# The expert stage of a routed feed-forward kernel: straight-line experts replaced by a looped body with a two-tile weight ring

## The reference, cut to what matters

```python
probs = softmax(xr @ Wg); gate_vals, expert_idx = top_k(probs, 2)      # 2048 tokens, 8 experts
C = ceil(1.25 * S * K / E)                                             # 640 slots an expert
dispatched = xr[dispatch_mask.reshape(-1) % S].reshape(E, C, d)        # rows of each expert
h = relu(einsum('ecd,edf->ecf', dispatched, w1))                       # w1: 8 x 512 x 2048, float32
expert_out = einsum('ecf,efd->ecd', h, w2)                             # w2: 8 x 2048 x 512, float32
out = einsum('ks,ksm->sm', combine_weights, rerouted); x = x + out     # two experts a token, gated
```

## Time and profile before

| What | Value |
|---|---|
| median of 3 runs | 1315.84 us |
| span of the profiled execution | 1310.3 us (5.5 us under the median, which has what lies around the span) |
| first part and routing | to 475 us |
| expert stage | 475 us to the end |
| instructions executed | 14966 |

### The profile page before, as it was taken

One profiled execution on the slowest core, in us unless ns is written; L12 is line 12 of the kernel. 1 busy time (PEld: TensorE's weight loads), 2 busy tenths in 40 slices (PEclk: granted clock), 3 DMA queues, 4 the chain that ended last, 5 costly groups with the idle time before them and its releaser, 6 DMA issues.

```text
span 1310.3 us, 14966 instructions
## 1 busy us (share of the span) xinstructions
PE 1061.0 (81%) x5058; PEld 837.0 (64%) x5059; DVE 656.6 (50%) x1010; ACT 488.9 (37%) x842; POOL 303.5 (23%) x242
## 2 busy tenths in 40 slices
PE   1055878877998359998997899999698994999895
PEld 0022335434465349997996799888586883988784
DVE  6989899899835223333332233334243432333342
ACT  5354736655644213322222222334243331233242
POOL 4767646476322300002001100100202002000202
PEclk9997997888899569998999899999798997999898
DMA  7051350220023341116221532163534332411441
GB/s 255 20 155 33 116 152 1 64 97 32 2 97 113 138 172 65 65 65 149 90 104 13 140 107 87 19 200 123 141 130 107 137 129 39 170 65 65 92 178 22
DMA packets 64617, 129.23 MB, mean 99 GB/s; under 512 B 4759, under 2 KB 4795, under 8 KB 64441
## 3 DMA queue, kind: packets, MB, share of 16 engines
q1 hardware_dynamic: 55784, 110.01, 24.7%
q0 software_dynamic: 8656, 17.13, 6.7%
HBM read 95.14 MB, written 35.22 MB: 99 GB/s over the span
## 4 chain that ended last, share of the span: by engine, by line
PE 57%; issue 6%; DMA 1%; POOL 1%; ACT 0%; DVE 0%; ACTq 0%; POOLq 0%; SPq 0%
PE ps_h L1117 9%; PE ps_y L1130 9%; PE ps_h L1118 9%; PE ps_y L1131 9%; PE ps_h L1119 9%; PE ps_y L1132 9%; PE ps_t L1096 1%; POOL out_dram L1076 1%; DMA rows<-slots 0%; DMA out_dram<-y,token 0%; PE ps_y L1096 0%; ACT y L1189 0%; DVE xl L1200 0%; ACT xh L1157 0%; ACTq L1003 0%
## 5 line engine op out<-in xcount | busy, mean ns | idle before, releaser
L1117 PE MATMUL ps_h<-xh,w1h 128*128 128x320 f32 (+3 forms) x768 | 250.7, 326 | 71.8 <-issue 71.8
L1118 PE MATMUL ps_h<-xl,w1h 128*128 128x320 f32 (+3 forms) x768 | 248.4, 323 | 3.7 <-issue 3.7
L1220 DVE SCALAR_TENSOR_TENSOR hl<-ps_h,hh 128x320 fp32r<-128x320 f32 (+3 forms) x192 | 95.2, 505 | 307.7 <-ACT hh L1174 307.7
L1119 PE MATMUL ps_h<-xh,w1l 128*128 128x320 f32 (+3 forms) x768 | 248.3, 323 | 0.0
L1076 POOL DMA_INDIRECT out_dram<-y,token x40 | 62.6, 1565 | 756.4 <-ACT y L1189 659.5
L1174 ACT ACTIVATE hh<-ps_h 128x320 fp32r<-128x320 f32 (+3 forms) x192 | 84.3, 451 | 358.6 <-PE ps_h L1119 358.6
L1130 PE MATMUL ps_y<-w2h,hh 128*128 128x512 f32 (+1 forms) x528 | 210.7, 399 | 1.4 <-DVE hl L1220 1.4
L1131 PE MATMUL ps_y<-w2h,hl 128*128 128x512 f32 (+1 forms) x528 | 207.0, 392 | 0.0
L1132 PE MATMUL ps_y<-w2l,hh 128*128 128x512 f32 (+1 forms) x528 | 206.4, 391 | 0.0
L1117 PEld LDWEIGHTS ps_h<-xh,w1h 128*128 128x128 f32 x768 | 150.0, 195 | 86.5 <-issue 78.1
L444 PE MATMUL ps_mm<-r1T,wm 128*128 (+1 forms) x320 | 164.2, 666 | 21.9 <-ACT z_in L606 15.0
(11 more groups left out here) (179 smaller groups left out, 1307.9 us busy)
## 6 DMA issues: line engine op xcount, KB each, us to landing
raw<-in_L_ffn_w_dram SPq DMA_DIRECT2D x66, 1024.0 KB, 7.5
slots<-r_rows SPq DMA_DIRECT2D x8, 1302.5 KB, 16.8
rows<-slots SPq DMA_DIRECT2D x8, 1302.5 KB, 6.0
f_rows<-in_fside_BxSxS_dram SPq DMA_DIRECT2D x5, 1024.0 KB, 5.4
rows<-in_x_dram SPq DMA_DIRECT2D x4, 1024.0 KB, 6.4
out_dram<-x_rows SPq DMA_DIRECT2D x4, 1024.0 KB, 5.2
slots<-r_rows POOLq DMA_DIRECT2D x1, 1302.5 KB, 6.7
rows<-slots SPq DMA_DIRECT2D x5, 260.5 KB, 3.6
```

Source lines behind the costliest of these rows:

```text
L1117: nc.tensor.matmul(o, w1h[r][:, dt, wcol], xh[:, par, dt, lo:hi], start=(dt == 0), stop=False)
L1118: nc.tensor.matmul(o, w1h[r][:, dt, wcol], xl[:, par, dt, lo:hi], start=False, stop=False)
L1119: last = nc.tensor.matmul(o, w1l[r][:, dt, wcol], xh[:, par, dt, lo:hi], start=False, stop=(dt == CT - 1))
L1220: v.scalar_tensor_tensor(out=hl[:, f % 2, lo:hi], in0=ps_h[:, bank, 0:hi - lo], scalar=0.0, in1=hh[:, f % 2, lo:hi].bitcast(F32), op0=ALU.max,
```

## The change: what it does

The expert's body becomes a loop. On PE each class has one body, used by even and odd experts; it holds up(0) and a loop of 8 rounds q over up(2q+1), down(2q), a turn for q = 2 to 6, up(2q+2), down(2q+1), with branches for the first and the last round. On ACT and DVE there are two bodies, up to 512 rows (always computed as 512) and over (always two times 320), each a loop over the 4 chunks.

The split weights are no longer whole chunks: w1h, w1l, w2h, w2l hold two hidden tiles each. In the step of hidden tile f, ACT and DVE split the w1 tile of f+2 and, once down(f-1) is through, the w2 tile of f+1.

`xh` and `xl` are there once. The next expert's rows are turned into `next_xh` and `next_xl` and copied over (128x2560 each, ACT and DVE) after relu 15. The next rows come by tiles of 128 into one `next_row`: SP asks for a tile when the one before is turned and its gate and token are read. SP's order for an expert is row tile 0, chunk loads 0 and 1, row tiles 1 and 2, chunk load 2, row tiles 3 and 4, chunk load 3, where chunk load c (for the chunk after next) waits until DVE has split the w2 tile of f = 4c+3. POOL copies each tile's token.

In the first part only the end differs: the counts are limited to 1 to 640, and three pieces of the first chunk are split there in place of eight. DVE clears `ps_h` once.

```diff
@@ experts, SP @@
+        def chunk(e, c):
+            sp.wait_ge(s_wl2, 16 * e + (4 * c + 4))
+            sp.nop(nofuse=True)
+            sp.wait_ge(s_w, 128 * e + 32 * (c + 2))
+            sp.nop(nofuse=True)
+            weights(sp, e + (c + 2) // NC, (c + 2) % NC, c % 2)
+        def row_tile(e, i):
+            if not (isinstance(e, int) and e == 0 and i == 0):
+                sp.wait_ge(s_tp, ST * (e + 1) + i)
+                sp.wait_ge(s_next_gate, ST * (e + 1) + i)
+                sp.wait_ge(s_next_token, ST * (e + 1) + i)
+            first = e * CAP + (CAP + i * P)
+            sp.dma_start(next_row[:], slots[bass.ds(first, P)]).then_inc(s_next, 16)
         def expert(e):
-            for c in range(NC):
-                sp.wait_ge(s_wl, PIECES * (e * NC + (c - 1)))
-                weights(e, c)
-                if c == 1:
-                    sp.wait_ge(s_tp, ST * (e + 1))
-                    load_slot_rows(sp, s_rows, rows, slots, e + 1)
+            row_tile(e, 0)
+            chunk(e, 0)
+            chunk(e, 1)
+            row_tile(e, 1)
+            row_tile(e, 2)
+            if not last:
+                chunk(e, 2)
+            row_tile(e, 3)
+            row_tile(e, 4)
+            if not last:
+                chunk(e, 3)
...
@@ experts, PE @@
         def turn(e, i):
-            pe.wait_ge(s_rows, 16 * (e + 1))
-            pe.wait_ge(s_xl, ST * e + i)
+            pe.wait_ge(s_next, 16 * ST * e + 16 * i + 48)
+            pe.wait_ge(s_xl, ST * (e + 1) + i)
...
-        with pe.Fori(0, NE // 2) as pair:
-            for par in range(2):
-                e = pair * 2 + par
-                def body(n):
-                    up(e, par, 0, n)
-                    for f in range(FT):
-                        if f + 1 < FT:
-                            up(e, par, f + 1, n)
-                        if f in TURN_AT:
-                            turn(e + 1, TURN_AT[f])
-                        down(e, f, n)
+        with pe.Fori(0, NE) as e:
+            def body(n):
+                pe.wait_ge(s_cur_h, e + 1)
+                pe.wait_ge(s_cur_l, e + 1)
+                up(e * FT, 0, n, first=True)
+                with pe.Fori(0, FT // 2) as q:
+                    at = e * FT + q * 2
+                    up(at + 1, 1, n)
+                    with pe.If(q < 1):
+                        pe.wait_ge(s_ya, e + 1)
+                        pe.wait_ge(s_yv, e + 1)
+                        down(at, 0, n, first=True)
+                    with pe.Else():
+                        down(at, 0, n)
+                    with pe.If(q < FT // 2 - 1):
+                        with pe.If(q > TURN_FROM - 1):
+                            turn(e, q - TURN_FROM)
+                        up(at + 2, 0, n)
+                        down(at + 1, 1, n)
+                    with pe.Else():
+                        down(at + 1, 1, n, last=True)
...
@@ experts, ACT (DVE alike, with the differences) @@
+        def split(e, c, j):
+            hidden = e * FT + c * FC + j
+            if j == 2:
+                act.wait_ge(s_w, 128 * e + 32 * c + 64)
+            a.activation(w1h[:, j % 2], raw1[...tile hidden + 2...], ACT.Copy).then_inc(s_wh1, 1)
+            act.wait_ge(s_f, hidden + 2)
+            a.activation(w2h[:, (j + 1) % 2], raw2[...tile hidden + 1...], ACT.Copy).then_inc(s_wh2, 1)
...
+                with act.Fori(0, NC) as c:
+                    for j in range(FC):
+                        if turned_before(j):
+                            with act.If(c > start - 1):
+                                token_high(e, tile_no(c * 2 + more))
+                        act.wait_ge(s_f, hidden + 1)
+                        ...relu to hh, 512 wide or 2 x 320...
+                        if j == FC - 1:
+                            with act.If(c > NC - 2):
+                                act.wait_ge(s_xh, ST * (e + 2))
+                                a.activation(xh[:], next_xh[:], ACT.Copy).then_inc(s_cur_h, 1)
+                        split(e, c, j)
```

More of the change, by code:

```diff
@@ L37 @@
 NC = FT // FC
-PIECES = 2 * FC
 W1C, W2C, U1C, U2C, BIN, BGATE, BOUT, BDEC, DBIAS = range(9)
@@ L106, in build_program, with load_chunk, first_pieces @@
             experts(nc, phase, ident, counts, rows, place0, load_sems, slots, out_rows, w1, w2)
-def load_chunk(sp, sems, raw1, raw2, w1, w2, e, c):
+def load_chunk(sp, sem, raw1, raw2, w1, w2, e, c):
     hidden = slice(c * FC * P, (c + 1) * FC * P)
[L112 to L136, removed]
+    sp.dma_start(raw1, w1[bass.ds(e, 1), :, hidden].rearrange("o (t p) f -> p (o t) f", p=P)).then_inc(sem, 16)
+    sp.dma_start(raw2, w2[bass.ds(e, 1), hidden, :].rearrange("o (t p) n -> p (o t) n", p=P)).then_inc(sem, 16)
+def first_pieces(place0):
+    raw1, raw2, w1h, w1l, w2h, w2l = place0
+    return ([(raw1[:, 0, :, n * P:(n + 1) * P], w1h[:, n], w1l[:, n], 0) for n in range(2)] +
+            [(raw2[:, 0, 0], w2h[:, 0], w2l[:, 0], 1)])
 def conditioning_and_routing(nc, ctx, ident, counts, rows, cond_buffers, gate_parts, place0, load_sems,
@@ L746, in _ @@
         act.wait_ge(load_sems[0], 32)
-        for piece in pieces(place0):
-            weight_high(nc, piece, load_sems[3])
+        for raw, high, _, which in first_pieces(place0):
+            a.activation(high, raw, ACT.Copy).then_inc(load_sems[2 + 2 * which], 1)
     @block.vector
@@ L969, in sem @@
         return ctx.enter_context(nc.semaphore(name))
[L973 to L977, removed]
+    raw1, raw2, w1h, w1l, w2h, w2l = place0
+    xh, xl = sb("xh", [P, CT, CAP], F32R), sb("xl", [P, CT, CAP], F32R)
@@ L991, in experts @@
+    s_ya, s_yv = sem("y_even"), sem("y_odd")
     s_gate, s_token, s_add = sem("gate_ready"), sem("token_ready"), sem("rows_added")
[L992 to L1014, removed]
@@ new lines, in expert @@
+        def expert(e, last):
+            row_tile(e, 0)
[9 more added lines that the diff above has]
+                chunk(e, 3)
+        sp.sem_inc(s_next, 32)
+        sp.wait_ge(s_w, 32)
+        weights(sp, 0, 1, 1)
+        expert(0, False)
+        with sp.Fori(1, NE - 1) as e:
+            expert(e, False)
@@ new lines, in up, with down @@
+                    nc.tensor.matmul(o, w1h[:, j, dt, :], xl[:, dt, lo:hi], start=False, stop=False)
+                    last = nc.tensor.matmul(o, w1l[:, j, dt, :], xh[:, dt, lo:hi], start=False, stop=(dt == CT - 1))
+                last.then_inc(s_h, 1 if wide else 2)
+        def down(hidden, j, n, first=False, last=False):
+            pe.wait_ge(s_wl2, hidden + 1)
+            pe.wait_ge(s_hl, 2 * hidden + 4)
+            for i in range(-(-n // P)):
+                m = min(P, n - i * P)
+                tok = slice(i * P, i * P + m)
+                nc.tensor.matmul(ps_y[0:m, i, :], hh[:, j, tok], w2h[:, j], start=first, stop=False)
+                nc.tensor.matmul(ps_y[0:m, i, :], hl[:, j, tok], w2h[:, j], start=False, stop=False)
+                done = nc.tensor.matmul(ps_y[0:m, i, :], hh[:, j, tok], w2l[:, j], start=False, stop=last)
+            done.then_inc(s_f, 1)
@@ new lines, in by_width, with tile_no, turned_before @@
+    def by_width(eng, e, body):
+        count = eng.value_load(counts[0:1, bass.ds(e, 1)], min_val=1, max_val=CAP)
+        with eng.If(count < WIDE + 1):
+            body(False)
+        with eng.Else():
+            body(True)
+    def tile_no(i):
+        return nc.s_assert_within(i, 0, ST - 1, skip_runtime_bounds_check_because=(
+            "the branch around it is taken from the first tile's turn on"))
+    def turned_before(j):
+        return {0: (-(1 + TURN_FROM // 2) - 1, 2), 2: (-TURN_FROM, 1)}.get(j)
```

299 lines of the change are left out of this document (158 added, 141 removed).

## The result

The changed kernel takes 1343.54 us (median of 4 runs, 1342.61 to 1344.94), the kernel before 1315.45 us beside it: a ratio of 1.0211 (95% interval 1.0195 to 1.0226), 28 us slower. 1348 had been predicted. The medians are only 28 us apart, because the profiled execution of before was a fast one: in every later run 1.6 to 1.9 us lie around the span (1344.39 us for 1342.7 here), and not 5.5 us, so its 1310.3 us stand for some 1312 us, about 3.4 us under the median.

A forecast was written before the change was run, and what follows sets the result against it. The prediction took the expert stage as bound by TensorE, with holes at expert boundaries; 88 + 21 + 3 - 3 - 77 = +32 us on 1310.3, plus 5.5 between span and median, gave 1348 us, range 1308 to 1400 (forecast's own 1325 to 1370).

The forecast's parts named there:

- Holes at the boundaries, removed: Between experts on PE: 64.5 us of idle time and 12.8 us of slow clock go, together 77 us.
- What comes back: At expert boundaries on PE: two cold jumps behind each expert of 640 rows, one or none elsewhere, 21 us with slow clock.
- Branches inside an expert: In PE's new loop: seven to nine branches a round at 0.08 us each, covered by PE's queue, costing nothing.
- ACT and DVE: At an expert's end: copying xh and xl makes DVE late for y in narrow experts, 3 us (0 to 8).
- The start: At entry to expert 0: two cold branches fall in smaller loads, 3 us less (0 to 7).
- Row tiles behind chunk loads: In SP's queue: row tiles 1 and 3 land late behind chunk loads 1 and 2, 63.7 us in 15 holes.
- the 8 us that I had named as a sign: Sign that the forecast is right: row tiles 1 and 3 land at 8 us and more, 2 and 4 near 3 to 4.
- Slow clock behind the holes: On PE behind the 15 row tile holes: 8 short ones at 1.4 us, 7 at 1.9 us, 24.5 us.
- Warm: Rival at the boundaries: all PE code stays in place, 5.6 us in place of 21, 1333 us; chance 0.15.
- cold: Rival at the boundaries: three cold jumps at every one, 69 us in place of 21, 1396 us; chance 0.12.
- exposed branches: Rival inside experts: PE's queue is too short behind waits, branches cost 45 us, 1393 us; chance 0.06.
- tile passes: Rival in the DMA queue: row tile does not wait for the 2 MB ahead, holes 11 us, 1271 us; chance 0.20.

The follow-up runs named there:

- e3_pe_code_twice: e1_tiles_ahead with PE's expert code written twice, for even and odd experts in a loop of four pairs; 1302.37 us, ratio 0.9896 to the kernel before.
- e6_five_classes: e1_tiles_ahead with five classes of row counts (320, 384, 512, 576, 640) in place of seven; 1232.09 us, ratio 0.937 to the kernel before.
- e5_short_copy: e1_tiles_ahead with the copies into xh and xl cut from 128x2560 to 4 x 8 columns, so later experts use old rows; 1238.74 us, ratio 0.9418.
- e4_pool_queue: The changed kernel with row tiles requested by POOL on its own DMA queue, at the same moments; 1308.51 us, ratio 0.995 to the kernel before.
- e1_tiles_ahead: The changed kernel with SP asking for row tiles 1 and 3 ahead of chunk loads 1 and 2; 1240.01 us, ratio 0.9427 to the kernel before.

## Why the prediction was right, point by point

- **Holes at the boundaries, removed: 77 us.** Right in kind, some 4 us short. The 64.5 us of idle time went (one hole of 4.9 us came back, counted below); e3_pe_code_twice shows that the amount of PE's code is enough to make them. The slow clock behind them was about 15 us and not 12.8, by the busy time of the stage (753.6 us before, 738.4 in e6_five_classes).
- **What comes back: 21 us.** Too high. One cold jump was left between experts, a hole of 4.9 us and 1 to 2 us of slow clock. The step that was mis-sized is the guess of two cold jumps behind each expert of 640 rows: the farthest code stayed in place too. The rule of the Trainium skill ("Runtime: NRT & Kernel Launch", Instruction fetch mechanics) that only a window of two pages is kept does not hold for PE here: jumps back over the 1540 instructions of the stage took 0.2 us. With the same section's 2048 instructions for PE two of the three sizes tried agree, none cold between experts at 1180 and many at 3080. The one cold jump at 1540 it does not foresee, and why that one is cold stays open.
- **Branches inside an expert: nothing.** Right. They cost 65 to 293 ns each, many of them about 0.2 us where I had taken 0.08, and no wait for "issue" appears inside an expert.
- **ACT and DVE: 3 us.** The sum of the waits is 4.3 us, so the size is right, but the cause is so for the smaller part only. The copies take 2.34 us on ACT (2.3 predicted) and 1.48 us on DVE (2.7 taken, 1.4 to 3.4 bounded), and e5_short_copy puts 0.7 us down to them; the rest is DVE at the end and start of an expert.
- **The start: 3 us.** 4.1 us earlier; the kernels of the experiments start theirs 2.5 to 5.0 us earlier. The two cold branches at the entry took 4.7 and 6.5 us in place of 6.8 and 7.5; that the smaller loads are the reason was not tried.
- **Row tiles behind chunk loads: 63.7 us in 15 holes.** The mechanism, the 15 places and their order by width are right; the sum is 73.4 us, since the tile of expert 4 came 10.5 us after down(5) in place of 10.2 (the chunk's first DMA went out after 1.9 us, not 1.6) and a period without its turn is shorter than the quarter that I took (3.8 against 4.1 us at 320 rows). From the chunk's first DMA the tile took 8.6 us, just as priced, and from its own issue 7.2 us, under the 8 us that I had named as a sign. The wait was priced as a queue in order; e4_pool_queue shows that the place in the queue is the smaller part of it, and the load beside the tile the larger. The number held because it was taken from two real DMAs of the same kind.
- **Slow clock behind the holes: 24.5 us.** Too low: 32.7 us by e1_tiles_ahead. I had priced short holes at 1.4 us; they cost as much as long ones: by the granted clock of the trace the half speed behind the eight holes under 4.1 us lasted 3.4 us six times and 6 us twice, behind the seven longer ones 2.8 to 6.1 us, and half of that is lost, 2.0 us on average for either kind (my estimate). Two windows of the changed kernel, behind a hole of 3.54 us in expert 1 and for as long again after it:

```profile
655.50:661.50 6.00, 5.97 (x24) 5.98 (x25) 1.25 (x3) 1.03 (x2) 0.35 (x2) 0.50 0.15 44
661.50:667.50 6.00, 6.00 (x34) 5.39 (x34) 1.87 (x3) 1.59 (x3) 0.01 (x1) 1.00 0.00 0
```

24 against 34 matmuls in 6.0 us is 1.8 us lost, and more in truth, since four of the 24 are the short transposes.
- **The sum.** The holes behind chunk loads cost 106 us (73.4 + 32.7) in place of 88, what came back was about 10 in place of 24, what went was about 81 in place of 77, and the start gave 4 in place of 3: 106 + 10 - 81 - 4 is +31, with rounding and a tail of 0.7 us the +32.4 of the two profiles. Each term had the right sign, but that errors of 18, 14 and 4 us left +32 as predicted is luck. So is a part of the last step: +32 was right between the profiles and 4 us too high between the medians, and of the 4.5 us that 1348 is too high 3.8 come from adding 5.5 us around the span where 1.7 lie. "Warm" was nearly the truth at the boundaries and would have said 1333 us with the holes as I had them; "cold" and "exposed branches" are refuted by the branch rows, "tile passes" by the 15 waits.

## What to carry to other kernels

Code that is run again should fit where the engine keeps it: here rolling the body took 55 us of holes away from PE (60.1 us of "issue" in the stage to 4.9), no such hole came up inside the loop, and doubling PE's code brought them back. When a load is split up, look at what each part stands behind in its queue's program: a small urgent transfer behind a large one that waits for something itself cost more than the whole gain (106 against 81 us), and two moved lines turned 2% slower into 6% faster. Price a hole in a matmul stage with the slow clock behind it.

## What the runs showed of the hardware

Very short holes can leave the granted clock alone. In e4_pool_queue the six holes of 1.7 to 2.2 us in experts 0 to 2 were followed by full clock, of which two stretches:

```profile
529.10:533.00 3.90, 3.87 (x28) 3.88 (x29) 1.25 (x3) 1.04 (x2) 0.55 (x1) 1.00 0.20 78
648.10:652.00 3.90, 3.90 (x28) 3.90 (x29) 1.24 (x3) 1.04 (x2) 0.61 (x1) 1.00 0.18 70
```

In the same kernel one of 1.85 us in expert 6 was followed by half clock, and so were all holes of 2.6 us and more; what tells the two apart was not tried. What a load costs a small transfer on another queue (5.6 to 6.5 us against 2.8 to 3.1) was the other thing that I had not expected.
